# A hybrid block of neighbourhood attention, full attention and a small FFN: key and value rows kept in a ring, half sums, wide strip scores, and an own order for the first image

## The reference

```
x = x + conv(group_norm(x))        # neighbourhood attention, 7 x 7 window, 16 heads of 8
    qkv = xf @ qkv_w.T
    logits[a, c] = sum_d q * k[si + a, sj + c] + rpb[...]    # 49 logits a point and head
    out = sum softmax(logits) * v[...];  y = out @ proj_w.T + proj_b
t = t + attn(layer_norm(t))        # full attention over 3136 points, 8 heads of 16
    softmax(q @ k.T / 4) @ v, then @ Wo + bo
t = t + (layer_norm(t) @ w_lora.T) @ W.T     # w_lora unpacked from 4-bit codes and scales
```

## Time and profile before

| | us |
|---|---|
| median of 3 runs | 9620.67 (9618.12 to 9624.71) |
| profiled execution | 9614.94 |
| its span | 9612.8 |
| PE busy | 8864.1 (92%) |
| DVE busy | 7885.6 (82%) |
| ACT busy | 6505.8 (68%) |
| POOL busy | 1829.3 (19%) |
| mean granted TensorE clock | 0.977 of full speed |

### The profile page before, as it was taken

One profiled execution on the slowest core, in us unless ns is written; L12 is line 12 of the kernel. 1 busy time (PEld: TensorE's weight loads), 2 busy tenths in 40 slices (PEclk: granted clock), 3 DMA queues, 4 the chain that ended last, 5 costly groups with the idle time before them and its releaser, 6 DMA issues.

```text
span 9612.8 us, 434952 instructions
## 1 busy us (share of the span) xinstructions
PE 8864.1 (92%) x173506; PEld 4432.8 (46%) x173506; DVE 7885.6 (82%) x14135; ACT 6505.8 (68%) x13345; POOL 1829.3 (19%) x1913
## 2 busy tenths in 40 slices
PE   4679999999999999999999999999999999999998
PEld 3434444444444444444444444444444444444543
DVE  4478888888888888888888888888888888889996
ACT  1247767767676666776767666676666766677777
POOL 4402221022211222112220122201222022210000
PEclk8779999999999999999999999999999999999999
DMA  2421221212112121121221112111121212111000
GB/s 57 67 52 29 38 39 34 48 33 37 36 32 49 34 38 32 49 35 33 39 39 43 33 35 41 36 47 34 33 37 36 54 27 36 38 39 31 8 10 8
DMA packets 516512, 354.32 MB, mean 37 GB/s; under 512 B 113245, under 2 KB 507213, under 8 KB 512461
## 3 DMA queue, kind: packets, MB, share of 16 engines
q1 hardware_dynamic: 514508, 325.98, 17.7%
HBM read 233.15 MB, written 78.05 MB: 32 GB/s over the span
## 4 chain that ended last, share of the span: by engine, by line
PE 81%; issue 9%; DVE 6%; ACT 2%; POOL 1%; SPq 1%; DMA 0%; DVEq 0%; ACTq 0%; POOLq 0%
PE PS L962 22%; PE PS L1041 20%; PE PS L1026 19%; PE PS L792 6%; PE PS L834 6%; PE PS L843 4%; DVE block_max L1469 3%; PE PS L853 3%; ACT PB L1242 1%; DVE PVM L1354 1%; PE PS L816 0%; DVE SUMS L1344 0%; DVE X L1401 0%; POOL SC L701 0%; DVE X L1369 0%
## 5 line engine op out<-in xcount | busy, mean ns | idle before, releaser
L1242 ACT ACTIVATE PB<-PS 128x448 f32<-128x448 f32 (+1 forms) x11200 | 5464.7, 544 | 2195.1 <-PE PS L1026 2163.9
L1469 DVE TENSOR_REDUCE block_max<-PS 128x1 f32<-128x448 f32 x10878 | 6141.6, 616 | 760.5 <-PE PS L962 698.8
L962 PE MATMUL PS<-KP,QP 96*32 96x448 bf16 x43904 | 4177.7, 359 | 162.2 <-issue 54.9
L1026 PE MATMUL PS<-QP,KP 99*32 99x448 bf16 x43904 | 4195.9, 355 | 100.1 <-ACT PB L1242 54.6
L1041 PE MATMUL PS<-PB,VA 128*32 128x448 f32 x22400 | 2680.8, 543 | 14.2 <-issue 12.8
L962 PEld LDWEIGHTS PS<-KP,QP 96*32 96x32 bf16 x43904 | 1279.1, 96 | 1941.4 <-DVE block_max L1469 880.4
L1026 PEld LDWEIGHTS PS<-QP,KP 99*32 99x32 bf16 x43904 | 1298.0, 97 | 1288.5 <-issue 536.3
L1041 PEld LDWEIGHTS PS<-PB,VA 128*32 128x32 f32 x22400 | 731.3, 111 | 372.1 <-issue 43.4
L701 POOL TENSOR_TENSOR SC<-SC,NM 128x1120 f32<-128x1120 f32 x224 | 461.9, 2062 | 2055.8 <-DVE NM L1340 2055.8
L706 POOL TENSOR_TENSOR SC<-SC,SUMS 128x1120 f32<-128x1120 f32 x224 | 462.0, 2062 | 1999.9 <-DVE SUMS L1349 1999.9
L834 PE MATMUL PS<-Kn,QB 32*32 32x80 f32 x25088 | 623.5, 237 | 163.8 <-issue 92.4
(11 more groups left out here) (99 smaller groups left out, 3796.3 us busy)
## 6 DMA issues: line engine op xcount, KB each, us to landing
VP<-vT_padded SPq DMA_DIRECT2D x1792, 70.0 KB
QP<-q_dram SPq DMA_DIRECT2D x672, 56.0 KB, 2.1
k_dram<-k_parts SPq DMA_DIRECT2D x56, 336.0 KB, 4.9
q_dram<-q_parts SPq DMA_DIRECT2D x56, 336.0 KB, 2.7
KP<-k_dram SPq DMA_DIRECT2D x336, 56.0 KB, 2.2
KP<-k_dram SPq DMA_DIRECT2D x48, 392.0 KB, 5.9
VA<-v_dram SPq DMA_DIRECT2D x16, 816.0 KB, 4.4
vT_padded<-VTs SPq DMA_DIRECT2D x112, 112.0 KB
```

Source lines behind the costliest of these rows:

```text
L962: ins = mm(PS[at:at + QT, bank, 0:BLK], QP[0:ROWS, Q_SLOTS[k % AUNITS], t:t + QT], KP[0:ROWS, g, t // BLK, j * BLK:(j + 1) * BLK], start=T ...
L1026: ins = mm(PS[k0:k0 + 32, bank, 0:BLK], KP[0:ROWSM, k // NBLK, h, c * P + k0:c * P + k0 + 32], QP[0:ROWSM, Q_SLOTS[k], h * BLK:(h + 1) * B ...
L1242: S.activation(exp_buffer(k, c)[0:n, h, :], PS[0:n, at % ST_BANKS, 0:BLK], ACT.Exp, scale=float(ADIM) ** -0.5).then_inc(exp_done, 1)
L1469: V.tensor_reduce(block_max[:, q, j:j + 1], PS[:, bank, 0:BLK], AX.X, ALU.max).then_inc(max_read, 1)
```

## The change

1. **Ring.** `KR` holds 8 rows of keys (row y in slot y % 8) instead of the whole image. POOL copies the rows that a strip adds from `Kn`, now two blocks (`roll_keys`). `load_windows` fetches only the added rows of values, two a strip as a rule in place of eight. The bias table gets 8 row types in place of 5, since the order of rows in the ring turns.
2. **Half sums.** In the loop POOL adds the two halves of a strip's exponentials into `HS` (`halve_sum`), DVE sums 560 elements a partition in place of 1120.
3. **Values.** The reading of the values' PSUM bank with the head mask moves from DVE to ACT (four activations of 112 elements), the gathering of heads from DVE to POOL (two additions, of 224 and 112 elements).
4. **Wide scores.** In the loop `QB` is 128 wide (all 16 heads), and each scores matmul takes all 128 channels at tile position (0, 32g). The first image keeps the narrow form.
5. **First image.** The DMAs of bias columns go ahead of most weight loads; the row DMAs (L500) go, DVE builds the table (`fill_table`) between the normalisations. Unpacking of the FFN weights is spread over later slots. `front_alone` is an own plan with a strip every 10 slots and four strip buffers (two of them in `PB`, idle until the loop). Its maxima tiles (`first_max`, 98 of unit 0 and 16 of unit 1) run as tasks inside the plan once keys and queries of a block are back. The engines no longer wait for the whole setup.

```
-ROW_TYPES = [0, 1, 2, STRIPS - 2, STRIPS - 1]
+ROW_TYPES = [0, 1, 2, 3, 4, 5, STRIPS - 2, STRIPS - 1]
 def max_step(m):
-    return m // NBLK, m % NBLK
+    return m % QTILES, m // QTILES
...
             self.fix(t + 5, 1, "exponentials", s)
-            self.fix(t + 6, 0, "sum_up", s)
+            self.fix(t + 6, 0, "halve_sum", s)
+            self.fix(t + 7, 0, "sum_up", s)
+            self.fix(t + 2 * PERIOD - 1, 1, "gather", s)
...
+            self.fix(t - 5, 1, "roll_keys", s)
...
+    def front_alone(self):
...
+        start, period = 24, 10
+        at = [start + period * s for s in range(STRIPS + 2)]
+        for s in range(STRIPS):
+            t = at[s]
+            for n in range(3):
+                self.fix(t + n, 0, "scores", 3 * s + n)
+            self.fix(t + 3, 0, "maxima", s)
+            self.fix(t - 3, 1, "roll_keys", s)
+            self.fix(t - 2, 0, "spread_queries", s)
+            self.fix(t + 4, 0, "subtract", s)
+            self.fix(t + 6, 0, "exponentials", s)
+            self.fix(t + 13, 1, "sum_up", s)
+            self.fix(t + 14, 0, "invert_strip", s)
+            self.fix(t + 15, 0, "normalise", s)
+            for c in range(4):
+                self.fix(t + 23 + c, 0, "turn", 4 * s + c)
+            self.fix(t + 19, 0, "load_windows", s)
+            self.fix(t + 28, 0, "values", s)
+            self.fix(t + 31, 0, "gather", s)
...
+            gap = (4 * period - 4) / len(tiles)
+            for n, (k, i, q) in enumerate(tiles):
+                self.place(t + 16 + int(gap * n), "first_max", (k, i, q))
...
 def load_windows(s):
-                    for ky in range(WI):
-                        src = bass.AP(tensor=vT_dram.tensor, offset=(row + ky) * (WIDE * P),
+                    for row in rows:
+                        src = bass.AP(tensor=vT_dram.tensor, offset=row * (WIDE * P),
...
 def scores(s, p, bank):
                     for u in range(u0, u1):
                         for g in range(4):
                             r = slice(32 * g, 32 * g + 32)
-                            ins = mm(PS[r, bank, (u - u0) * KEYS:(u - u0 + 1) * KEYS], QB[r, u, :],
-                                     k_img[r, row:row + WI, u * QJ:u * QJ + WJ], start=True, stop=True,
-                                     tile_position=(32 * g, 32 * g))
+                            ins = mm(PS[r, bank, (u - u0) * KEYS:(u - u0 + 1) * KEYS], QB[:, u, r],
+                                     KR[:, :, u * QJ:u * QJ + WJ], start=True, stop=True, tile_position=(0, 32 * g))
...
+                def values(s, bank):
+                    act.wait_ge(pv_in, of(b, ahead, STRIPS, s + 1))
+                    for h in range(GH):
+                        ins = S.activation(PVM[:, h, :, :], pv[:, h, :, :], ACT.Copy, scale=head_mask[:, h:h + 1])
+                def halve_sum(s):
+                    pool.wait_ge(exps, of(b, ahead, STRIPS, s + 1))
+                    G.tensor_tensor(HS[:, :, :], SC[:, s % 2, :, 0:KEYS // 2], SC[:, s % 2, :, KEYS // 2:KEYS],
+                                    ALU.add).then_inc(sum_halved, 1)
+                def gather(s):
+                    pool.wait_ge(masked, of(b, ahead, STRIPS, s + 1))
+                    G.tensor_tensor(PVM[:, 0:2, :, :], PVM[:, 0:2, :, :], PVM[:, 2:4, :, :], ALU.add).then_inc(paired, 1)
+                    G.tensor_tensor(o, v[:, 0, :, :, :], v[:, 1, :, :, :], ALU.add).then_inc(out_strip, 1)
```

More of the change, by code:

```diff
@@ L116, in __init__ @@
                 self.fix(17, 1, "load_x", 1)
-        if front:
+        if front and attention:
             self.front()
+        elif front:
+            self.front_alone()
         self.order = [self.taken[key] for key in sorted(self.taken)]
+        self.maxima = [i for task, i in self.order if task == "first_max"]
     def tails(self, attention):
@@ L222, in window_row, with row_type, ring_runs, table_runs @@
     return min(max(QI * strip - KSZ // 2, 0), SIDE - WI)
+def row_type(strip):
+    return strip if strip < 2 else 2 + (strip - 2) % 4 if strip < STRIPS - 2 else strip - STRIPS + len(ROW_TYPES)
+def ring_runs(rows):
+    runs = []
+    for row in rows:
+        if runs and row % WI == runs[-1][1] + runs[-1][2]:
+            runs[-1][2] += 1
+        else:
+            runs.append([row, row % WI, 1])
+    return runs
+def table_runs(kind):
+    s = ROW_TYPES[kind]
+    runs = []
+    for w in range(WI):
+        row, ys = window_row(s) + w, []
+        for i in range(QI * s, QI * s + QI):
+            at = first_key(i) - window_row(s)
+            ys.append(first_key(i) - i + KSZ - 1 + w - at if at <= w < at + KSZ else 2 * KSZ - 1)
+        slot = row % WI
+        if runs and slot == runs[-1][0] + runs[-1][1] and all(
+                y == first + runs[-1][1] and y < 2 * KSZ - 1 for y, first in zip(ys, runs[-1][2])):
+            runs[-1][1] += 1
+        else:
+            runs.append([slot, 1, ys])
+    return runs
+def new_rows(strip):
+    row = window_row(strip)
+    return range(row if strip == 0 else max(row, window_row(strip - 1) + WI), row + WI)
+def windows_loaded(strip):
+    return sum(len(new_rows(n)) for n in range(strip % 2, strip + 1, 2))
 def first_key(i):
@@ L425, in side_read @@
                 return ffn_out, of(b, third(i), NBLK, i + 1)
+            if task == "first_max":
+                return max_read, alone.maxima.index(i) + 1
+            if task == "combine":
+                return setup_dve, len(NF4) + 3
             assert task == "turn_max"
@@ L1186, in do @@
                         turn(i // 4, i % 4, bank)
+                    elif task == "values":
+                        values(i, bank)
                     elif task == "square2":
@@ L1437, in do @@
                         invert_strip(i)
-                    elif task == "values":
-                        values(i, bank)
                     elif task == "proj":
```

424 lines of the change are left out of this document (273 added, 151 removed).

## The result

The changed kernel takes 9308.6 us (median of 4 runs, 9303.1 to 9311.1), the kernel before beside it 9619.4 (4 runs, 9615.3 to 9624.7): a ratio of 0.9676, 95% interval 0.9659 to 0.9693. Forecast were 9305. The sum came out, its terms did not: the front gave 101 us where 158 were expected, the loop 206 where 155 were.

The account below looks back on a forecast made before the run. PE was taken to bound the loop, DVE next, and the front to be a chain of waits. Savings of 158 (front) and 155 (loop), 313, from 9614.9 gave 9302, said as 9305; range 9230 to 9380, 8 in 10 9190 to 9430.

Parts of the forecast that it names:

- The start: Front, up to the first scores: they move from 91.4 to about 43 to 45, saving 48 us (35 to 55).
- The strips: Front, 27 strips: a cycle through PE, DVE and POOL shortens from 13.14 to 11.7 us each, saving 39 (-12 to 74).
- rival A: Front's strips: the cycle doesn't shorten, PE stays cold and becomes the bound at 13.6, part gives -12; 9356 us; chance 0.16.
- Behind the last strip: Front, from the last values to the loop: 119.7 us become 48, saving 71 (55 to 80).
- The bound of 55: Lower bound of the saving behind the last strip, if the shift DMA lands only when the large loads drain.
- wide scores: Loop, PE's scores: shorter pieces and no 0.10 entry gap save 100 us (59 to 143).
- DVE's relief less ACT's reads: Loop: fewer PE waits for DVE give 40 us (0 to 90), ACT's four added reads cost 15 (0 to 212).
- ring: Loop: 6 of 8 window loads go, part of PE's `issue` waits with them, saving 30 us (0 to 90).
- rival C: PE's scores in the loop: four wide matmuls of one unit don't overlap, loop slower than before, from 0.26 a unit; chance 0.05.
- all but 15: Loop: ACT's four reads, 0.27 each and 212 us in all, hide but for 15 us.
- rival D: POOL comes late in the loop, so the change is worth only the front: 9462 us; chance 0.10.
- its own signs: Profile marks of being right, such as first scores near 44 and loop start near 430; wrong: a front above 480.

Follow-up runs that it names:

- the shorter memset: On top of early spreading and the early shift, POOL writes KP's ones as 12544 f32 words instead of 25088 bf16: 9263.1 us, ratio 0.9609 to the kernel before.
- early spreading: Changed kernel with the next strip's key rolling and query spreading ahead of POOL's subtraction, first image only: 9241.4 us, ratio 0.9598 to the kernel before.
- the shift first: Changed kernel with the shift's three small DMAs issued ahead of the loads of group 1 keys and values: 9291.1 us, ratio 0.9650 to the kernel before.
- the two runs with all rows: Changed kernel loading all eight value rows for every strip: 9392.9 us; the same with window loads four chunks later: 9342.4 us.
- the eight kernels with two loads a strip: The changed kernel and those altering only the front or the time of the window loads, same loop code: loops of 8793 to 8841 us by their profiles.
- full sums: Changed kernel with DVE summing all 1120 elements in the loop and no half sums on POOL: 9309.3 us, ratio 0.9674 to the kernel before.

## Why the prediction was right, and where only its sum was

**The start: 36.8, not 48.** The step said that DVE stops at the first `fill_table` until 21, when the columns have landed. That holds: with the shorter memset, where nothing else keeps DVE, they have landed by 20.13. But the statistics come 49 us earlier than before, and the normalisation behind them now meets POOL's memset of KP. In the kernel before the memset held only a step of unpacking, with time to spare. This wait is a term that the step does not have. DVE was free at 28.87, 8 us later than the step has it. From there to the first scores it takes 25.8, where I had 22 to 24: the stores run one behind the other, most of them 3.15 apart, as forecast, and the first waits for its values.

**The strips: 4.9, not 39. This step failed.** The cycle was named rightly, since breaking it at its one avoidable link (spreading behind `subtract`) gave 42 us in the strips; its length was wrong in two terms. First, from the spread to the maximum I had 3.96 or 2.6 for the scores, 1.9 for DVE and handovers, some 4.7 to 6.1. In the 21 strips without any splitting on POOL it is 5.4 to 8.1, on average 6.7; with POOL's 5.5 that makes 12.2. In the strip of the POOL rows it is 7.9 (110.34 to 118.24), near the longest. The timelines of PE and of DVE in it:

```profile
110.44 2.98 PE L1016 MATMUL PS<-KR,QB 32*32 32x80 f32 x80 [4.59 <-POOL QB L837]
113.34 1.72 PE L966 MATMUL PS<-XN,W_qkv 128*32 128x448 f32 x8
114.99 1.07 PE L1016 MATMUL PS<-KR,QB 32*32 32x80 f32 x32
```

```profile
116.25 0.56 DVE L1556 TENSOR_TENSOR SC<-PS,nat_bias 128x240 f32<-128x240 f32 x2
116.84 1.32 DVE L1565 TENSOR_REDUCE NM<-SC 128x14 f32<-128x1120 f32 x1
```

The scores and DVE's part have the lengths of the step (2.98 and 1.07; 1.9). What it lacks is the projection of the next block between the second and the third piece, 1.65 us of PE inside the cycle, which I had counted as work beside it. Six of the 21 strips have it there and take 7.5 on average; the other 15, with shorter tasks of other strips and blocks between their pieces or none, take 6.4. Second, POOL's splitting of keys and queries does not fit where POOL waits. Measured between second spreads, the five strips that hold most of it take 16.3, the other 22 take 12.1; 5 x 4.2 = 21 us, over 27 strips 0.8 each. With 12.1 in place of 11.7 (11 us) that is 32 of the 34 us that are missing. The clock rose from 0.78 to 0.82 only: rival A had named it as the cause for strips that stay as they are, and was nearer to their size (-12) than the forecast (39). The cause was the cycle: with early spreading the clock is 0.88 in the same stretch (54.6 to 387.9), PE's work 252 us instead of 267, on the same number of instructions: the clock rose because the waits went, and not the other way round.

**Behind the last strip: 59.6, not 71.** The table cuts at the scores of strip 27, the step at the last strip's values. By the step's cut 119.7 us become 55.7 (430.0 to 485.7), where it has 48: 64.0 saved. The other 4.4 are lost between the scores of strip 27 and its values (21.1 us before, 25.5 after), which no term of the sum has. The bound of 55 was written down with its reason, that the shift DMA lands only when the large loads drain. That is what happened: with the shift first, the 55.7 are 42.5. The wait cost 13 us, and the rest of the step had been put 5 too high.

**The loop: 206, not 155.** Undone one by one:

| | forecast | measured, loop |
|---|---|---|
| wide scores | 100 (59 to 143) | 76 |
| DVE's relief less ACT's reads | 25 | 46 (values), 2 (half sums) |
| ring | 30 (0 to 90) | 54 |
| sum | 155 | 178 |

Each has its forecast's sign, and each lies in its range. The 2 of the half sums is nothing that the runs resolve, and the ring's 54 may be up to 14 higher, since its profile is of the fastest of its executions. The remaining 28 of 206 belong to none of the four and are within the scatter of the loop. The order in which the loop takes its maxima changed too (`max_step`), and no run undoes that. The wide form's gap went entirely, as the earlier trace rows let expect, and the piece of five takes 0.71, near the 0.68 at best: 0.142 a unit, where rival C decides from 0.26 on. That the weight loads of the wide form hold its matmuls up doesn't show either: in the piece of 2029.21 PEld has the 40 loads for 0.89 from 2029.03 on, PE the 40 records of the matmuls for 0.90 from 2029.21 on, so they run side by side. The runs favour the wide form by 76 us. ACT's reads cost 0.355 each, 1.42 a strip and 278 us in all, and PE waits less for ACT than before (71.2 after 83.9): as far as the waits show, all of it is hidden, not all but 15. POOL's load goes from 19% to 30% of the span, and PE's waits for POOL are 0.3 us of the 8000: rival D's did not come. The ring gave more, since the eight loads of a strip fell together with its scores: DMAs that nobody waits for still held PE up, as the two runs with all rows show (`issue` at the scores 48.7 us in 8000, with the same loads four chunks later 22.7, in the changed kernel 21.9). By what means they do it, no run shows.

So the forecast hit by 4 us because its two errors have opposite signs: 57 too much in the front, 51 too little in the loop. That the total fits so well is luck. Of its own signs, the front was to be ready near 430 (it is 485.7, above the 480 that I had called wrong), a strip to come every 11 to 12 us (12.96), the first scores near 44 (54.6), and DVE's share lower by 4 points (2: 82% to 80%). In the loop its signs came: no gap of 0.10 ahead of the wide scores and 0.71 in them. By the front's signs it was wrong, by the total right.

## What to carry to other kernels

When two engines form a cycle through a queue, write down each engine's whole queue between the two ends of the link, also the tasks that belong to others: they are in the cycle. Then look for the one step that waits only because of where it stands; moving it here was two lines and took 42 us out of the strips. When work is moved earlier, look at what already runs there, on the other engines and in the DMA queues too: here POOL's memset made 13.29 us of a DVE operation of 0.51. And when a small DMA releases a stage, issue it ahead of the large ones (the loop began 3.7 us after that issue here, in place of 16.8).

## What the runs showed of the hardware

- A POOL memset of 32 x 25088 bf16 takes 21.0 us, of the same bytes as 12544 f32 words 10.55: its time goes by elements. A DVE `TENSOR_SCALAR` on 128 x 448 f32 that meets it is held to its end (13.29 and 3.03 us in place of 0.51), and one on 128 x 128 int32 in the kernel before too (8.02 in place of 0.23); `BN_STATS` beside it keeps its 3.79 for seven.
- Matmuls of K 128 and rows of ten elements in 80 columns run at 0.71 us for 40 records on four column groups, faster than four 32 x 32 tiles a unit (0.83, the median of such pieces before), and 0.19 behind the tile ahead of them, where those start at 0.29. The 40 weight loads of such a piece (0.89) run beside its matmuls (0.90).
- PE loses time as `issue` where DMAs that it doesn't wait for are issued. At the strip's scores it is 18.9 to 21.9 us in 8000 in the eight kernels with two loads a strip, 48.7 with eight loads beside the scores, 22.7 with the same loads four chunks later. Over all lines it is 148 to 175, 210 and 185; the 185 shows nothing by itself, since full sums, with two loads, have 187.
- POOL's operations on two inputs cost less an element the wider they are, but not evenly: 3.8 ns at 112 (L866), 2.96 at 224 (L862), 2.49 at 560 (L853), 1.91 at 896 (L846), 1.84 at 1120 (L872), but 2.53 at 224 where the queries are spread (567 ns). The slope that I drew between 224 and 1120 for the spreading missed the half sums by 0.2 us.
